# Routed experts in unsplit f32, and one-hot tiles weighted by GpSimd in every other step

## What is computed

```python
x = x + neural_memory(layernorm(x))        # gradients, updated weights, read
x = x + experts(x, ...)                    # product-key experts, first time
x = x + causal_attention(layernorm(x))     # 16 heads, low-rank projections
y = x + experts(x, ...)                    # the same experts again

def experts(x):                            # n tokens, d = 256, 8 heads, 64 keys a side
    q = batchnorm(x) @ w_q.T
    sx, ix = top_k(q_x @ keys_x, 8); sy, iy = top_k(q_y @ keys_y, 8)
    scores, pk = top_k(sx[:, None] + sy[None, :], 8); idx = (ix * 64 + iy)[pk]
    o = gelu(x @ key_in[idx].T) * softmax(scores)
    return o @ key_out[idx]
```

## Time and profile before

| | |
|---|---|
| median of 3 runs | 3398.86 us |
| profiled execution, its own time | 3402.41 us |
| its span, first to last instruction | 3400.6 us, granted TensorE clock 0.975 |
| gradient stage and memory read | 0 to about 315 us |
| first expert stage | about 315 to 1300 us; `weigh` of chunk 0 at 369.07, of chunk 15 at 1237.50 |
| attention and its projections | about 1300 to 2410 us |
| second expert stage | about 2410 to 3400 us; `weigh` of chunk 15 at 3333.74, last `weigh` at 3368.36 |
| one chunk in the middle of a stage | 57.9 us |

### The profile page before, as it was taken

The page is one execution under the profiler, slowest core; times in us unless marked ns, Lnnn a source line. Parts: engine busy times, 40 slices in busy tenths (PEclk is TensorE's granted clock), DMA queues, the critical chain, the costliest instruction groups (busy, mean ns, idle before and its releaser), DMA issues. The chain is left out here.

```text
span 3400.6 us, 74937 instructions
## 1 busy us (share of the span) xinstructions
PE 3180.5 (94%) x29442; PEld 2235.4 (66%) x29442; DVE 2876.6 (85%) x8980; ACT 1644.9 (48%) x2256; POOL 677.0 (20%) x357
## 2 busy tenths in 40 slices
PE   8998799999999988799999999998789999999997
PEld 7886588888888867333333333334568888888886
DVE  5757899999999996788888888882799999999996
ACT  4534444444444434346556656565344444444441
POOL 0000233333333340200000000000033333333333
PEclk9998999999999999799999999998899999999999
DMA  4225000000000005631212111003300000000000
GB/s 154 80 60 161 10 15 11 20 11 20 11 20 11 17 8 167 166 64 34 37 33 51 34 34 36 8 6 113 102 8 11 20 11 20 11 20 11 20 8 17
DMA packets 130869, 140.56 MB, mean 41 GB/s; under 512 B 29974, under 2 KB 115926, under 8 KB 130518
## 3 DMA queue, kind: packets, MB, share of 16 engines
q1 hardware_dynamic: 120918, 126.72, 14.1%
q10 hardware_dynamic: 9600, 9.05, 0.9%
HBM read 84.75 MB, written 50.59 MB: 40 GB/s over the span
## 5 line engine op out<-in xcount | busy, mean ns | idle before, releaser
L490 PE MATMUL f_p_route<-f_x_w,f_y_hot 128*128 128x64 f16 x8192 | 902.4, 194 | 54.1 <-DVE f_weighted L768 42.9
L514 PE MATMUL f_p_out<-kout_in,f_hidden 128*128 128x256 f16 x6144 | 853.7, 273 | 17.5 <-POOL f_hidden L408 16.5
L503 PE MATMUL f_p_hid<-f_xtc,kin_in 128*128 128x256 f16 x6144 | 856.0, 274 | 5.9 <-ACT f_hidden L604 5.8
L408 POOL TENSOR_TENSOR f_hidden<-f_weighted,f_hidden 128x1024 f16<-128x1024 f32 x256 | 612.5, 2393 | 1217.4 <-DVE f_x_w L758 1213.2
L2066 DVE TENSOR_REDUCE at_part_max<-at_p_ring 128x1 f32<-128x512 f32 (+3 forms) x1280 | 706.1, 603 | 113.0 <-PE at_p_ring L1945 74.8
L490 PEld LDWEIGHTS f_p_route<-f_x_w,f_y_hot 128*128 128x128 f16 x8192 | 697.2, 98 | 96.2 <-issue 60.9
L514 PEld LDWEIGHTS f_p_out<-kout_in,f_hidden 128*128 128x128 f16 x6144 | 600.0, 98 | 196.0 <-issue 118.6
L503 PEld LDWEIGHTS f_p_hid<-f_xtc,kin_in 128*128 128x128 f16 x6144 | 602.4, 98 | 80.0 <-issue 10.1
L609 ACT CAST f_hidden<-f_weighted 128x1024 f16<-128x1024 f32 x256 | 342.9, 1340 | 465.3 <-DVE f_weighted L768 465.3
L604 ACT ACTIVATE f_hidden<-f_p_hid 128x512 f32<-128x512 f32 x512 | 301.9, 596 | 500.5 <-PE f_p_hid L503 497.3
L1945 PE MATMUL at_p_ring<-at_k,at_q 96*128 96x512 bf16 (+3 forms) x1280 | 416.3, 362 | 40.0 <-DVE at_m_rest L2083 15.4
(11 more groups left out here) (272 smaller groups left out, 3451.1 us busy)
## 6 DMA issues: line engine op xcount, KB each, us to landing
at_q<-qk SPq DMA_DIRECT2D x42, 256.0 KB, 4.5
at_k<-qk SPq DMA_DIRECT2D x42, 256.0 KB, 4.3
x<-f_ln_y SPq DMA_DIRECT2D x32, 256.0 KB, 2.8
xt<-f_ln_xt SPq DMA_DIRECT2D x32, 256.0 KB, 3.6
f_xt_in<-xt SPq DMA_DIRECT2D x32, 256.0 KB, 2.8
f_xres<-x SPq DMA_DIRECT2D x32, 256.0 KB, 2.7
qk<-ap_parts_q SPq DMA_DIRECT2D x16, 384.0 KB, 3.8
qk<-ap_parts_k SPq DMA_DIRECT2D x16, 384.0 KB, 5.0
```

The costliest lines, as they stand in the source:

```text
L408: nc.gpsimd.tensor_tensor(lo, weighted[s % WR], hi, ALU.subtract).then_inc(lo_ready, 1)
L490: last = nc.tensor.matmul(p_route[:, t, :], y_hot[:, s % HR, t // PAIR, :, t % PAIR], x_w[:, s % HR, half, t // PAIR, :, t % PAIR], start= ...
L503: last = nc.tensor.matmul(p_hid[g % 2][:, xp % 2, :], kin_t[:, a, dh, xp * P:(xp + 1) * P], xt[slot][:, b, dh, :], start=i % 6 == 0, stop= ...
L514: last = nc.tensor.matmul(p_out[:, u, :], parts[slot][:, xp, u * P:(u + 1) * P, a], kout[:, b, xp, :], start=g == 0 and i == 0, stop=xp == ...
```

## The change

The expert products take f32 operands in one matmul: `expert_in` and `expert_out` have 4 matmuls a group in place of 12, and the f16 parts, the ring `weighted`, `copy_xt`, `split_xt`, `round_weighted` and `split_weighted` are gone. `weigh` multiplies `hidden` in place. The splits of `key_in` and `key_out` are gone; `key_out` is loaded into its place by DMA. The tokens have three buffers (`XR`), and each is loaded when its last reader is two chunks past. `hot` gets two buffers, and in steps 1, 3, 5 and 7 (`GP_STEPS`) the product `x_w` is made by GpSimd instead of VectorE. TensorE waits for it by a new semaphore `tiles_shared`.

```diff
-HR, WR = 2, 2
+HR, XR = 2, 3
+GP_STEPS = tuple(range(1, NS, 2))
...
-            def split_weighted(c, slot, s):
-                pool.wait_ge(hi_ready, ONE + c * NS + s + 1)
-                if s + 2 < NS or s + 1 < NS and exists(c + 1):
-
-                    pool.wait_ge(hot_ready, ONE + c * NS + s + 3)
-                hi, lo = step_parts(slot, s)
-                nc.gpsimd.tensor_tensor(lo, weighted[s % WR], hi, ALU.subtract).then_inc(lo_ready, 1)
...
+            def share_tiles(c, slot, s):
+                pool.wait_ge(p_lo_ready, ONE + c + 1)
+                pool.wait_ge(hot_steps, ONE + c * NS + s + 1)
+                above(pool, route_ready, c * NS + s + 1 - HR)
+                nc.gpsimd.tensor_tensor(x_w[:, s % HR, :, :, :, :], hot[:, s % HR, :, :, :].unsqueeze(1).to_broadcast(BOTH),
+                                        shares_of(slot, s), ALU.mult).then_inc(tiles_shared, 1)
+
+            for c in range(NCH):
+                for s in GP_STEPS:
+                    share_tiles(c, c % 2, s)
...
                 if j == 0:
                     pe.wait_ge(hot_ready, ONE + c * NS + s + 1)
+                    if s in GP_STEPS:
+                        pe.wait_ge(tiles_shared, ONE + gp_steps_below(c * NS + s + 1))
...
-            EXPERT_STEPS = 12
+            EXPERT_STEPS = 4
...
-                xp, dh, (a, b) = 2 * g + i // 6, i % 6 // 3, PAIRS[i % 3]
-                last = nc.tensor.matmul(p_hid[g % 2][:, xp % 2, :], kin_t[:, a, dh, xp * P:(xp + 1) * P], xt[slot][:, b, dh, :],
-                                        start=i % 6 == 0, stop=i % 6 == 5)
+                xp, dh = 2 * g + i // DH, i % DH
+                last = nc.tensor.matmul(p_hid[g % 2][:, xp % 2, :], kin_t[:, dh, xp * P:(xp + 1) * P], xt[c % XR][:, dh, :],
+                                        start=dh == 0, stop=dh == DH - 1)
...
-                            for i in range(j % PS * 3 // 4, (j % PS + 1) * 3 // 4):
+                            for i in range(j % PS // 4, (j % PS + 1) // 4):
...
+                if s in GP_STEPS:
+                    above(dve, tiles_shared, gp_steps_below(c * NS + s + 1 - HR))
+                nc.vector.tensor_tensor(hot[:, s % HR, :, :, :], y_iota[:, 0:2 * NX, :].unsqueeze(1).to_broadcast(wide), tokens(xq[slot], wide),
                                         ALU.is_equal).then_inc(hot_steps, 1)
-                nc.vector.tensor_tensor(y_hot[:, s % HR, :, :, :], y_iota[:].unsqueeze(1).to_broadcast(tall), tokens(yq[slot], tall),
-                                        ALU.is_equal)
-                dve.wait_ge(hot_steps, ONE + c * NS + s + 1)
...
+                last = nc.vector.tensor_tensor(y_hot[:, s % HR, :, :, :], y_iota[:].unsqueeze(1).to_broadcast(tall), tokens(yq[slot], tall),
+                                               ALU.is_equal)
+                if s not in GP_STEPS:
+                    dve.wait_ge(hot_steps, ONE + c * NS + s + 1)
+                    if s == 0:
+                        dve.wait_ge(p_lo_ready, ONE + c + 1)
+                    last = nc.vector.tensor_tensor(x_w[:, s % HR, :, :, :, :], hot[:, s % HR, :, :, :].unsqueeze(1).to_broadcast(BOTH),
+                                                   shares_of(slot, s), ALU.mult)
+                last.then_inc(hot_ready, 1)
...
-                nc.vector.tensor_tensor(weighted[s % WR], h, p_route[:].rearrange("p t (u x) -> p x u t", u=2),
+                nc.vector.tensor_tensor(h, h, p_route[:].rearrange("p t (u x) -> p x u t", u=2),
                                         ALU.mult).then_inc(routed, 1)
```

More of the change, by code:

```diff
@@ L303, in pb @@
             return ctx.enter_context(nc.psum_tensor(tag + name, shape, F32))
-        parts = [h[:].rearrange("p x t -> p (x t)").bitcast(F16).rearrange("p (x t k) -> p x t k", x=NX, k=2) for h in hidden]
-        xt = [sb(f"xtc{b}", [P, 2, DH, CH], F16) for b in range(2)]
+        xt = [xt_in] + [sb(f"xtc{b}", [P, DH, CH]) for b in range(XR - 1)]
         xn = sb("xn", [P, DH, CH])
@@ L329, in routed_experts @@
         y_hot = sb("y_hot", [P, HR, PS // PAIR, P, PAIR], F16)
-        hot = sb("hot", [P, PS // PAIR, 2 * NX, PAIR], F16)
+        hot = sb("hot", [P, HR, PS // PAIR, 2 * NX, PAIR], F16)
         x_w = sb("x_w", [P, HR, 2, PS // PAIR, 2 * NX, PAIR], F16)
-        ring = [sb(f"weighted{i}", [P, NX * 2 * PS]) for i in range(WR)]
-        weighted = [r[:].rearrange("p (x u t) -> p x u t", x=NX, u=2) for r in ring]
         xres = sb("xres", [P, 2, D])
@@ L383, in exists, with gp_steps_below @@
             return not isinstance(c, int) or 0 <= c < NCH
+        def gp_steps_below(k):
+            return len([i for i in range(k) if i % NS in GP_STEPS])
         block = ctx.enter_context(nc.Block())
@@ L395, in _ @@
                            allow_small_or_imprecise_dtypes=True).then_inc(iota_ready, 1)
-            def split_xt(c, slot):
-                pool.wait_ge(xt_copied, ONE + c + 1)
-                nc.gpsimd.tensor_tensor(xt[slot][:, 1, :, :], xt_in[:], xt[slot][:, 0, :, :], ALU.subtract).then_inc(xt_lo_ready, 1)
-            def split_weighted(c, slot, s):
-                pool.wait_ge(hi_ready, ONE + c * NS + s + 1)
-                if s + 2 < NS or s + 1 < NS and exists(c + 1):
-                    pool.wait_ge(hot_ready, ONE + c * NS + s + 3)
-                hi, lo = step_parts(slot, s)
-                nc.gpsimd.tensor_tensor(lo, weighted[s % WR], hi, ALU.subtract).then_inc(lo_ready, 1)
-            def one(c, slot):
-                for s in range(NS):
-                    split_weighted(c, slot, s)
-                    if s == XT_AT and exists(c + 2):
-                        split_xt(c + 2, slot)
-            split_xt(0, 0)
-            split_xt(1, 1)
             if ahead is not None:
@@ L509, in expert_out @@
                 if i == 0 and g == 0:
-                    pe.wait_ge(lo_ready, ONE + c * NS + NS)
+                    pe.wait_ge(routed, ONE + c * NS + NS)
                     above(pe, y_ready, c)
-                xp, u, (a, b) = 2 * g + i // 6, i % 6 // 3, PAIRS[i % 3]
-                last = nc.tensor.matmul(p_out[:, u, :], parts[slot][:, xp, u * P:(u + 1) * P, a], kout[:, b, xp, :],
-                                        start=g == 0 and i == 0, stop=xp == NX - 1 and i % 3 == 2,
+                xp, u = 2 * g + i // 2, i % 2
+                last = nc.tensor.matmul(p_out[:, u, :], hidden[slot][:, xp, u * P:(u + 1) * P], kout[:, xp, :],
+                                        start=g == 0 and i == 0, stop=xp == NX - 1,
                                         skip_group_check=True)
@@ L594, in copy_picks @@
                 above(act, hot_ready, (c - 1) * NS)
+                above(act, tiles_shared, (c - 1) * len(GP_STEPS))
                 nc.scalar.activation(xq[slot][:], p_picks[:, 0, :], ACT.Identity, bias=tile_base[:])
@@ L744, in one_hots @@
                 wide, tall = [P, PS // PAIR, 2 * NX, PAIR], [P, PS // PAIR, P, PAIR]
-                both = [P, 2, PS // PAIR, 2 * NX, PAIR]
                 def tokens(tile, shape):
@@ L969, in load_kout @@
             def load_kout(j):
-                above(sp, kout_lo, j - SLOTS + 1)
-                sp.dma_start(kout[j % SLOTS][:], key_out.rearrange("(x y) d -> y x d", y=P)[:, j * XG:(j + 1) * XG, :]).then_inc(
-                    kout_loaded[j % SLOTS], 16)
+                sp.dma_start(kout_t[:, j * XG:(j + 1) * XG, :], key_out.rearrange("(x y) d -> y x d", y=P)[:, j * XG:(j + 1) * XG, :]).then_inc(
+                    kout_loaded, 16)
             for c in range(RX):
@@ L1008, in _ @@
                 sp.wait_ge(xt_stored[b], ONE + 16 * len(range(b, NCH, RT)))
+            sp.wait_ge(kout_loaded, ONE + 16 * N_KOUT)
             sp.wait_ge(s["xln_ready"], ONE + NCH)
@@ L1213, in step @@
                     prepare(n - 5)
-                    if kout_item(n - 5) is not None:
-                        round_kout(kout_item(n - 5))
                 if valid(n + 2):
```

88 lines of the change are left out of this document (25 added, 63 removed).

## The result

| | before | changed |
|---|---|---|
| median | 3398.88 us (3397.81 to 3402.24, four runs) | **3889.66 us** (3888.43 to 3892.15, four runs) |
| ratio | | 1.1443 (95% interval 1.1423 to 1.1463) |
| profiled execution | 3402.41, span 3400.6 | span 3888.2 |
| one middle chunk | 57.9 us | 75.35 us |

The forecast was 3489 us, with a range of 3285 to 3585. The kernel became slower, as forecast, but by 491 us and not by 90, and it lies 305 us above the range.

A forecast was written before the change was run, and what follows sets the result against it. TensorE bounds, VectorE 5% behind; the bound moves to VectorE, held by GpSimd, at 61.8 us a chunk. Per stage 58.5 + 5 - 6.5 = +57, twice +114, ends -23.5: +90, so 3489 us; range 3285 to 3585.

The forecast's parts named there:

- Cost of the matmuls: TensorE, expert stages: 128 f32 matmuls at 0.216 us replace 384 split ones, 27.6 us a chunk for 41.9.
- about 3950: Rival: an f32 matmul costs four f16 ones, TensorE needs 76.5 us a chunk and bounds; chance 0.01.
- Bare f32 weight loads: TensorE, routing mixes: 0.08 us of f32 weight load bare behind a routing matmul, eight times a step, 5.1 us a chunk.
- VectorE's own work: VectorE: four x_w leave (4.6 us) and 0.5 us of waits for GpSimd go, leaving 50 us a chunk.
- GpSimd's product: GpSimd's x_w of 2048 elements takes 4.7 us; ends 2.4 us (f16 inputs twice as fast) and 6 us.
- The hold on VectorE: While GpSimd's product runs, VectorE instructions with two SBUF inputs are blocked; candidates of step 0 waits from 1.1 to 4.5 us.
- y_hot stays ahead of GpSimd: In odd steps y_hot is already running when GpSimd is released by hot, so it finishes first, still at 1.22 us.
- The third rival: GpSimd's product gets ahead of y_hot, VectorE stands 4.6 us four times a chunk: 3750 us; chance 0.14 with the slow-product case.
- The walk: Step-by-step timing of one expert-stage chunk with blocked VectorE and waits for routing: next chunk at 59.9 us, against 57.9.
- The clock: TensorE's idles before route(3) and route(7) bring the lower clock: 1.9 us more a chunk, making 61.8 us.
- Ends of the stages: Each stage's start -6.5 us, its last chunk +5; the last expert_outs -10.9 and -12.6 us.
- Edits at nothing: Removed splits of key_in and key_out, and ScalarE's and GpSimd's other splits, hidden behind other work: counted as nothing.

The follow-up runs named there:

- the added products: Changed kernel with one more f32 product of 256 columns in each of expert_out's 16 groups a chunk: 4107.73 us, ratio 1.2082.
- the late wait: Changed kernel with half of the expert matmuls left out, GpSimd's product waiting for the end of y_hot instead of hot: 3385.49 us, ratio 0.995.
- the kernel with half of the products: Changed kernel with half of the expert matmuls left out (64 f32 matmuls a chunk remain), GpSimd's part kept: 3347.35 us, ratio 0.9843.

## Why the prediction was wrong

**The step that failed is "Cost of the matmuls": "An f32 product thus costs two f16 ones, not three: 0.216 for 0.327 us".** The 0.216 us was read rightly as the distance of two *rows*, and taken for the cost of a *matmul of the program*. The run of the earlier trace rows is L1121 with x4, which the forecast called four matmuls; the loop at that line runs over two halves of the features, and the program has two matmuls there. The same trace had more of it: L471's f_p_sim has 512 rows where `sub_scores` has 4 matmuls a call, 2 calls a chunk, 32 chunks, 256 in all. This is its group in the kernel before:

```profile
L471 PE MATMUL f_p_sim<-wct_in,f_xn 128*128 128x512 f32 x512 | 267.7, 613 | 23.7 <-ACT f_xn L567 18.1
```

A count of rows against the loop would have given 0.432 us, so 55.3 us a chunk for 128 products where 27.6 were put, and 41.9 before: **+13.4 us a chunk instead of -14.3**. With that the forecast's own sum for TensorE, 57.7-41.9+55.3+5.1, is 76.2 us; 75.35 were measured. The error of 27.7 us a chunk would be 830 us if TensorE had bounded in both readings; the forecast of 61.8 us was bounded by VectorE, so only 13.6 us of it showed in a middle chunk. The whole miss is 401 us.

**A rule that said so was cited and put aside for a wrong reason.** The Trainium skill, page "FP8 and Floating Point Precision", section "TensorE Precision Notes", says true FP32 takes four passes. The forecast cited it, worked out 55.8 us a chunk from it, and gave it 0.01, since "The row shows two, not four". There were two rows of two f16 costs each, four in all: the trace agrees with that rule (0.432 us by the run's starts, 0.426 by the added products, against 4 x 0.109). The forecast's rival on this ground, "about 3950", was within 2% of 3889.66. A number that so contradicts a stated rule should have been counted once more before the chance went to 0.01.

Point by point, the rest:

- **Bare f32 weight loads:** 5.1 us a chunk forecast; 8 x 0.08 us in each mix, and 4.5 us by moving the matmuls, which took away 56 of the 64. Right. The 0.119 us of the earlier trace rows is a row's too (64 rows for 32 matmuls), but here the row was the right unit: of a product's two weight loads only the first stands behind a short routing matmul.
- **VectorE's own work:** 50 us forecast, 203.48/4 = 50.9 measured.
- **GpSimd's product:** 4.7 us forecast, 3.61 measured. The earlier trace rows have one f32 and one f16 input (a value and its high part), 2.33 ns an element; the product, with two f16 inputs, takes 1.76. So it did go faster than those rows, by a quarter and not by half as the 2.4 us end had it; whether the type or the repeated elements do it was not tested. With its wait of 0.86 us (1 us forecast) the row shows 4.47, by chance near 4.7.
- **The hold on VectorE:** right as a mechanism (`candidates` 2.96 us, and 3.24 with the late wait, for 0.69), but the forecast's 3.4 us of blocked time were half too much against 2.3. In the changed kernel it is nearly all hidden under TensorE.
- **y_hot stays ahead of GpSimd:** right, 1210 to 1225 ns in all 256 steps. The third rival did not happen.
- **The walk:** in the kernel with half of the products a chunk takes 56.05 us at the full clock where the walk had 59.9. From `weigh` to `weigh` the excess stands where GpSimd's end counts: step 0 took 9.0 us for 10.1, step 2 7.1 for 8.0, step 3 5.4 for 5.9, step 6 6.9 for 8.0. The product ended 1 us earlier than the walk said, and a mix with four f32 matmuls is some 0.3 us shorter than one with eight at 0.216. That kernel came out at 0.984, more by the stages' ends than by its middle chunks, which at 57.67 us are about even with 57.9.
- **The clock:** TensorE has no idle in a middle chunk of the changed kernel, and 1.00 is granted. The 1.9 us a chunk had no place there. In the kernel with half of the products the fallen clock costs 1.6 us a chunk, so as a mechanism it was right.
- **Ends of the stages:** forecast -6.5 at each start, +5 for each last chunk, -23.5 for the last `expert_out`s. The first and the last rested on the cheap product. Measured: +3.2 at the first start, +11.6 between the stages, +3.0 at the end, and -0.2 for each last chunk. 64 matmuls of 0.432 are 27.6 us where the split ones took 21.14 and 22.80. In the kernel with half of the products, whose blocks take what the forecast said, the same stretches are -9.4 (for -6.5), -15.8 (for -6.5-10.9) and -11.5 (for -12.6), with +1.6 and +2.1 for the last chunks.
- **Edits at nothing:** the splits that went saved nothing to be seen; the start of the first stage is 3.2 us later all the same.

**The direction was luck.** The forecast's reason, that GpSimd holds VectorE, costs almost nothing in this kernel (5.9 us); it counts only where VectorE bounds (+84.9 us), and less than forecast. The kernel nearest to the forecast's own picture, with half of the products, takes 3347.35 us where the kernel before takes 3401.16: faster. Its chunk is below the 58.8 us, and its product below the 4.0 us, under which the forecast itself expected a gain. So with f32 products at 0.216 us "slower" would most likely have been wrong, though no run here has exactly that load.

What made the kernel slower is that the product it came to save on costs four f16 products, where three were used.

## What to carry to other kernels

Before a duration is taken from a trace, divide the count of its rows by the count of that matmul in the program: an f32 matmul stood as two rows here, and a run "x4" can be two instructions. A product in f32 costs four f16 ones here, so a split in three is cheaper than f32 unsplit, and one f16 product (if its precision will do) cheaper than both; among short f16 matmuls an f32 one also lays its weight load bare. Work given to GpSimd next to a full VectorE held up VectorE's instructions with two SBUF operands here, and whatever stood behind it in GpSimd's own order was late by the whole of it. And where a forecast's sign hangs on a term of a few us, a stand-in kernel that has the load of the forecast shows whether the sign was earned.
